# Zero stores and weight loads of an attention stage issued in pieces, and its first tile list built one sequence sooner, in a fused four-part kernel on one core

## The reference, cut to what matters

```
def _L0_cond_ref(...):     # one of 8 dense FFNs for each sequence (argmax of cond_8)
    ...
def _L0_ffn_ref(x, ...):   # attention and a mixture of 8 experts
    h = x + _gqa(_rmsnorm(x, attn_norm_w), wq, wk, wv, wo)     # 16 heads of 16, 4 key heads, causal
    out = h + _moe(_rmsnorm(h, ffn_norm_w), gate_w, expert_w)  # each token: its top 2 of 8 matrices 256x256
    return out
def _L1_cond_ref(...):     # base matrix and 8 low-rank ones, weighted by cond_8
    ...
def _L1_ffn_ref(...):      # 16 experts of width 512 that pick 128 tokens each a group, and a shared expert
    ...
x = x + _L0_ffn_ref(_L0_cond_ref(x, ...), ...)
x = x + _L1_ffn_ref(_L1_cond_ref(x, ...), ...)
```

## Time and profile before

| what | us |
|---|---|
| median of 3 runs | 2167.01 |
| lowest and highest of the runs | 2162.46, 9101.47 |
| the profiled execution | 2170.83 |
| its span | 2169.2 |
| TensorE busy in the span | 2057.0 |
| VectorE, ScalarE, GpSimd busy | 1356.1, 1116.4, 961.7 |

### The profile page before, as it was taken

How to read it: one execution, slowest core, us unless ns; L and a number is a source line. 1 busy time by engine, 2 the same in 40 slices (tenths; PEclk the granted TensorE clock), 3 DMA queues, 4 the chain that set the end, 5 groups by cost and what they waited for, 6 DMA issues and landing times. The chain is left out here.

```text
span 2169.2 us, 48239 instructions
## 1 busy us (share of the span) xinstructions
PE 2057.0 (95%) x16360; PEld 1753.8 (81%) x16392; DVE 1356.1 (63%) x2815; ACT 1116.4 (51%) x2216; POOL 961.7 (44%) x1062
## 2 busy tenths in 40 slices
PE   6999968899999999997997999999989999999997
PEld 6999965566666666665996999999978888888886
DVE  6888844466767676675554776788754454544452
ACT  6777733466666666654563333344345444445452
POOL 0000002245555555564754444444345656565653
PEclk9999987799999999997998999999999999999998
DMA  7767711312322232224984444454345454545442
GB/s 254 266 252 261 263 63 26 108 58 95 93 90 78 94 92 78 91 80 152 312 291 155 154 150 138 153 180 137 112 112 117 91 116 89 116 89 116 91 85 30
DMA packets 133511, 289.09 MB, mean 133 GB/s; under 512 B 22897, under 2 KB 64626, under 8 KB 126962
## 3 DMA queue, kind: packets, MB, share of 16 engines
q1 hardware_dynamic: 83314, 176.98, 24.7%
q0 software_dynamic: 50048, 110.14, 20.1%
HBM read 186.90 MB, written 95.42 MB: 130 GB/s over the span
## 5 line engine op out<-in xcount | busy, mean ns | idle before, releaser
L1049 DVE TENSOR_REDUCE neg_max<-ring 128x2 f32<-128x512 f32 (+1 forms) x384 | 250.5, 683 | 101.7 <-remote 72.5
L820 POOL TENSOR_SCALAR_AFFINE_SELECT weights_diag<-weights_diag 128x512 f32<-128x512 f32 x256 | 157.0, 638 | 287.2 <-ACT weights_diag L932 287.0
L2746 POOL DMA_INDIRECT out<-eo,row_put x128 | 201.2, 1572 | 161.4 <-ACT eo L2810 136.5
L2884 DVE TENSOR_TENSOR ex_hid<-ex_up_ps,gelu 128x512 f32<-128x512 f32 x128 | 87.0, 689 | 172.2 <-ACT gelu L2794 172.2
L2794 ACT ACTIVATE gelu<-ex_gate_ps 128x512 f32<-128x512 f32 x128 | 76.2, 596 | 187.3 <-PE ex_up_ps L62 187.3
L2216 POOL DMA_INDIRECT picked_rows<-results,lo_row_now x128 | 133.3, 1041 | 56.0 <-issue 29.5
L932 ACT ACTIVATE weights_diag<-ring 128x512 f32<-128x512 f32 x256 | 138.4, 599 | 31.5 <-PE ring L1567 31.5
L60 PE MATMUL ex_down_ps<-ex_dn_lo,ex_hid_hi 128*128 128x256 f32 x512 | 145.2, 284 | 2.8 <-issue 2.8
L61 PE MATMUL ex_down_ps<-ex_dn_hi,ex_hid_lo 128*128 128x256 f32 x512 | 145.6, 284 | 0.0
L62 PE MATMUL ex_down_ps<-ex_dn_hi,ex_hid_hi 128*128 128x256 f32 x512 | 145.0, 283 | 0.0
L828 POOL DMA_INDIRECT sorted_rows<-h_sb,row_now x128 | 127.2, 993 | 33.0 <-issue 31.4
(11 more groups left out here) (397 smaller groups left out, 7539.8 us busy)
## 6 DMA issues: line engine op xcount, KB each, us to landing
ug_raw<-in_w_ug SPq DMA_DIRECT2D x32, 1028.0 KB, 5.0
dn_raw<-in_w_dn SPq DMA_DIRECT2D x32, 640.0 KB, 5.2
q_t<-sorted_rows SPq DMA_DIRECT2D x136, 128.0 KB, 3.3
moe_w<-in_expert_gu SPq DMA_DIRECT2D x16, 1024.0 KB, 4.8
results<-c0n POOLq DMA_DIRECT2D x33, 256.0 KB
x_raw<-in_x_t SPq DMA_DIRECT2D x32, 256.0 KB, 5.1
c0n<-c SPq DMA_DIRECT2D x32, 256.0 KB, 4.4
c0r<-c SPq DMA_DIRECT2D x32, 256.0 KB
```

Source lines behind the costliest of these rows:

```text
L820: nc.gpsimd.affine_select(part, part, [[0, G], [1, P]], ALU.is_ge, 0.0, base=0, channel_multiplier=-1).then_inc(kept_done, 1)
L1049: nc.vector.tensor_reduce(out, src, AX_X, ALU.max, negate=True).then_inc(max_done, 1)
L2746: nc.gpsimd.indirect_dma_start(out=out_rows, out_offset=bass.IndirectOffsetOnAxis(ap=at, axis=0), in_=eo[c][:, n, :], in_offset=None, comp ...
L2884: nc.vector.tensor_tensor(hid[f % 2][:], up_ps[f % 2][:], gelu[f % 2][:], ALU.mult).then_inc(hid_done, 1)
```

## The change

SP no longer issues the eight zero stores and the five loads in body 2. One zero store is issued at the end of each of the bodies 4 to 11, behind `move_odd_heads`, and one load at the end of each of the bodies 12 to 23: eight parts of `moe_w` of 256 KB (`WE_PARTS`), then the four small weights. ScalarE waits for 128 on `routes.we_in` instead of 16. VectorE's `count_a` moves to body 30, behind `maxima(31, 0, 3)`, `place_a(0)` to the end of body 30, behind `keep_shares` and ahead of the weight parts; `place_a(1)` and `words_a` stay in body 31, one after the other, in the place where `count_a` stood.

```
-            def clear_spare_tiles():
-                sp.wait_ge(zeros_set, 1)
-                for e in range(EM):
-                    at_ = EM * REGION + e * P
-                    sp.dma_start(sorted_rows[at_:at_ + P, :], zeros[:]).then_inc(zeros_out, 16)
+            def clear_spare_tile(e):
+                if e == 0:
+                    sp.wait_ge(zeros_set, 1)
+                at_ = EM * REGION + e * P
+                sp.dma_start(sorted_rows[at_:at_ + P, :], zeros[:]).then_inc(zeros_out, 16)
+
+            def load_later(n):
+                if n < WE_PARTS:
+                    sp.dma_start(part_of(routes.we, n), part_of(we_source, n)).then_inc(routes.we_in, 16)
+                else:
+                    dst, src, arrived = later_weights[n - WE_PARTS]
+                    sp.dma_start(dst[:], src).then_inc(arrived, 16)
...
-                if i[1] == 2:
-                    clear_spare_tiles()
-                    for dst, src, arrived in later_weights:
-                        sp.dma_start(dst[:], src).then_inc(arrived, 16)
...
                 if exists(later(i, 2)):
                     move_odd_heads(i)
+                if 0 <= i[1] - 4 < EM:
+                    clear_spare_tile(i[1] - 4)
+                if 0 <= i[1] - 12 < WE_PARTS + len(later_weights):
+                    load_later(i[1] - 12)
...
-                    act.wait_ge(routes.we_in, 16)
+                    act.wait_ge(routes.we_in, 16 * WE_PARTS)
...
                 if is_at(i, B - 1):
-                    count_a()
+                    place_a(1)
+                    words_a()
                 if rows_:
                     rows_to_scatter(m_rows)
...
                 if rows_:
                     keep_rows(m_rows)
+                if is_at(i, B - 2):
+                    count_a()
...
-                if is_at(i, B - 1):
-                    place_a(0)
                 if has_h:
                     h_low(i)
...
-                if is_at(i, B - 1):
-                    place_a(1)
...
-                if is_at(i, B - 1):
-                    words_a()
+                if is_at(i, B - 2):
+                    place_a(0)
                 for part in weight_parts(i):
```

More of the change, by code:

```diff
@@ L473, with attention_phase @@
 RULES = 64 + EM * EM
-def attention_phase(nc, sem, c0, at, x, sums, sorted_rows, results, routes, shared, later_weights, shared_sources, ended):
+def attention_phase(nc, sem, c0, at, x, sums, sorted_rows, results, routes, shared, we_source, later_weights, shared_sources, ended):
     with ExitStack() as ctx:
@@ L631, in attention_phase @@
         LIST_A, LIST_B, MOVES = 20, 27, 39
+        WE_PARTS = 8
         PICKS, ROWS = 17, 4
@@ L3025, in block_program @@
             attention_phase(nc, passing_later_sem, c0, at, t["x"], sums, sorted_rows, results, routes, shared,
-                            [(routes.we, t["moe_w"], moe_w_in), *((dst, t[n], shared.const_in) for dst, n in ((shared.b_raw, "lora_b"), (shared.wb, "w_base"), (shared.bb, "b_base"), (shared.cond, "cond_er")))],
+                            t["moe_w"], [*((dst, t[n], shared.const_in) for dst, n in ((shared.b_raw, "lora_b"), (shared.wb, "w_base"), (shared.bb, "b_base"), (shared.cond, "cond_er")))],
                             [t[n] for n in ("shared_gu", "shared_d", "lora_a", "route_w")], passing)
```

## The result

The changed kernel took 2147.43 us in the median of four runs (2145.74 to 2148.75), the kernel before 2164.79 in the median of its four beside it (its first three gave 2167.01). The ratio is 0.9921 with a 95% interval of 0.9909 to 0.9934: 17 us less, clear of the noise and far inside 2%. One of the four runs before took 9101.47 us and counts in both of its medians; the middle of the other three is 2162.57, which would make it 15 us. The changed kernel run again later, five runs beside nine of the kernel before (e0_after_again), gives 16.6. Forecast: 2146.4, range 2139 to 2158. The time was met, in part by luck: the largest term was too large by 5 us, and other errors took most of that back.

A forecast was written before the change was run, and what follows sets the result against it. TensorE, busy 95% of the span, bounds the kernel, so time comes only from its idle stretches or clock. -17.7 + 0 + 0.9 + 4.1 - 2.8 - 5.1 + 0 = -20.6 from 2167.0 gives 2146.4 us, range 2139 to 2158.

The forecast's parts named there:

- The burst (-17.7): Body 2: without SP's burst ahead of the shift, TensorE's 7.25 us stop and the low clock behind it go; -17.7 us.
- the lower bound of -7.3: Body 2: the burst's gain if the clock would fall there anyway; -7.3 us.
- The price of 0.43 us a us of low clock: Work behind body 2's stop: each us of work at 1.2 GHz loses 0.43 us, from 10.5/24.2.
- The pieces (0): Bodies 4 to 23: one more SP issue at each body's end is hidden in a 3.6 us gap; 0 us.
- the bound of 4 us: Bodies 4 to 23: upper bound for the twenty pieces, 0.2 us a body, making 4 us.
- rival (d): Twelve later pieces each hold up the next shift and the clock falls; slower, 101 us more, 2247 us; chance 0.03.
- count_a (+0.9): Body 30: its 2.6 us overflow VectorE's 1.72 us idle time and delay TensorE; +0.9 us, bounds 0 and +2.6.
- place_a(0) (+4.1): End of body 30: all of it delays body 31's residual, its two instructions taking 0.97 and 3.16; +4.1 us.
- The row of 3.16 us: Profiled time of place_a(0)'s second instruction beside four GpSimd selects, taken as due again in its new place.
- h_low (-2.8): Body 31: without place_a(0) ahead of h_low, the 2.79 us idle time before the gate goes; -2.8 us.
- the rows (-5.1): Change of stage: with the list a body earlier, TensorE's 5.08 us wait for the first rows goes whole; -5.1 us.
- The clock at the end (0): End of the stage: the clock falls earlier than now, for a similar amount of work; 0 us, bounds -4.7 and +4.

The follow-up runs named there:

- e1: Changed kernel with VectorE's order (tile list) put back as in the kernel before, SP's pieces kept; 2158.68 us, ratio 0.9941 to the kernel before.
- e3: Changed kernel with only the eight zero stores (1.0 MB) back as a burst ahead of body 2's shift; ratio 0.9907 to the kernel before.
- e4: Changed kernel with the whole burst (3.5 MB, 13 issues) back in body 2, but behind its shift; ratio 0.9910 to the kernel before.
- b1_before_again: The kernel before, unedited, profiled a second time; span 2164.1 us, bodies 2 to 4 in 71.31 us.
- b2_before_third: The kernel before, unedited, profiled a third time; span 2166.7 us, bodies 2 to 4 in 71.20 us.
- e2_list_only: Changed kernel with the burst back in body 2, so only VectorE's list is moved; 2161.03 us, ratio 0.9952 to the kernel before.
- e5: Changed kernel with four loads a body in bodies 12 to 14 in place of one in 12 to 23; ratio 0.9922 to the kernel before.
- e6: Changed kernel with place_a(0) moved into VectorE's idle time in body 30, behind the second round's fourth maxima; 2143.68 us, ratio 0.9898 to the kernel before.
- e8: Changed kernel with place_a(0) in body 30's idle time, count_a in body 29, place_a(1) and words_a in body 30; 2149.87 us, ratio 0.9932.

## Why the prediction was right, and where it was not

**The burst (-17.7).** Mechanism right: the shift waited behind it, the stop took the clock down, and with the burst gone nothing else stops body 2 (e1, e3, e4). The size came from one execution whose low clock lasted unusually long (its 59.5 us for three undisturbed bodies was nearly right: 58.85). The same step from b1_before_again, b2_before_third or e2_list_only gives 11.9 to 12.4. The failed step is the sentence that took the excess of one profile as the term, with the fall's full tail; the lower bound of -7.3 took in the right value. The price of 0.43 us a us of low clock held: b1 lost 12.4 - 8.0 = 4.4 us over 9.7, 0.45 a us.

**The pieces (0).** Right: 397.67 against 397.69 us for twenty bodies. e5 shows four times the load in one body still free, so the bound of 4 us was loose, and rival (d) far off.

**count_a (+0.9).** It took 949.90 to 953.63, 3.7 us and not 2.6, because two of its small instructions met GpSimd (1.44 us for one that took 0.23 before). That put 1.15 us of wait on TensorE. Within the bound of 2.6.

**place_a(0) (+4.1).** Its two instructions took 0.94 + 1.30 = 2.2 us, and TensorE's wait for the residual grew by 2.4 (0.98 to 3.35): near the estimate by the Trainium skill's rule, 2.6, and not by the row. The rule ("SBUF — State Buffer", Who interferes with whom: the one that starts first keeps the port for its whole instruction) fits this trace: L1230 starts within the first select and takes 0.36 us more than its 0.94 in e6. The four selects beside it grew from 3.23 to 4.57 us in turn. The row of 3.16 us was real (e1 repeats it at 3.17) but of another situation: there all four selects had their exponentials done and ran back to back in 2.40 us, while at the end of body 30 they are released one by one by ScalarE, and VectorE gets in between. That this is the reason was not tried by itself.

**h_low (-2.8) and the rows (-5.1).** Both waits went whole. List and loads were early enough: 7.5 us. e8, with the list earlier still, gained nothing by it, though its delayed maxima would hide a small gain.

**The clock at the end (0).** It fell during the residual's wait, as expected, but was soon back: the windows of 1 us of the changed kernel read 0.55 for 973 to 974, 0.74 for 976 to 977, and after a second short dip

```profile
983.00:984.00 1.00, 0.83 (x4) 0.59 (x4) 0.11 (x1) 0.95 (x2) 0.94 (x1) 0.67 0.63 199
986.00:987.00 1.00, 1.00 (x10) 1.00 (x7) 0.00 (x0) 0.83 (x2) 0.51 (x1) 0.62 0.71 226
```

that is about 6 us of work at 1.2 GHz in place of 10.9 (10.4 by the busy time in the windows).

The prediction overlooked a third low stretch. It expected the full clock up to about 970, but in body 30 it falls in both kernels at the wait of 1.76 us for the maxima, from 972.9 to 983.2 before and from 956.0 to 966.3 after:

```profile
972.00:973.00 1.00, 0.00 (x0) 0.00 (x0) 1.00 (x4) 0.00 (x0) 0.77 (x1) 0.97 0.00 0
983.00:984.00 1.00, 1.00 (x12) 0.06 (x4) 0.50 (x1) 0.47 (x1) 0.00 (x0) 0.91 0.00 0
```
```profile
956.00:957.00 1.00, 0.00 (x0) 0.00 (x0) 1.00 (x3) 0.00 (x0) 0.98 (x2) 0.52 0.20 70
966.00:967.00 1.00, 1.00 (x11) 0.36 (x9) 0.00 (x0) 0.46 (x1) 0.00 (x0) 0.86 0.00 0
```

It lasts 10.2 us in both and so hardly enters the difference between these two traces; in b1_before_again and b2_before_third it came 2 us behind that wait and lasted 6.8. By the price above some 4 us are still lost there, an estimate, which no edit here took up.

**The sum.** From the marks, with 71.2 us for bodies 2 to 4 before: 12.4 for the burst, 3.4 to 4.6 up to the first tile (5.0 against e1_pieces_only). These 16 to 17 us match the medians; in "sorted" and "rest" a difference is not to be told from their spread. The forecast of -20.6 was too large by 5.3 for the burst and too small by 0.5 to 1.7 for the list, and it was taken from 2167.0, a median of three runs into which the one of 9101.47 counts, and which on four runs is 2164.8. So 2146.4 stood 1 us from 2147.4 by luck, with a term that was off by 5. The prediction's remark that 2% is about what a measurement can tell from no change was too coarse: the interval of the ratio is some 3 us to either side.

## What to carry to other kernels

Put bulk transfers behind, not ahead of, a small move that the bounding engine waits for; whether they are split matters little as long as what stands ahead of the small move, its issues as well as its bytes, is through when the move is due. Before a stop's price is taken from a profile, look at a second execution: its wait repeats within 1 us, the low-clock tail behind it doesn't. When work is moved on an engine that is not the bound, look in the timeline for a stretch in which it waits for the bounding engine, and not for the place that comes early: the same two instructions cost 2.3 us of waiting at the end of body 30 and none some eleven us sooner.

## What the runs showed that was not expected

In single executions a shorter stop can cost more than a longer one: 3.78 us of wait with 24 us at 1.2 GHz (14.8 us together), 8.00 us of wait with 13.6 us (12.4). In five falls after a wait for the shift the low clock lasted 13.6, 13.6, 13.7, 24 and 27 us from fall to rise. What makes it long or short no run here shows.

The second `place_a(0)` instruction, 768 elements in one partition, took 0.94 to 0.95 us where no select had started before it, 1.30 with selects released one by one, and 3.16 and 3.17 behind four selects in a row, although it touches one partition of 128.
